# The split state of a pair-feature stage: through DRAM and back, or copied by GpSimd into a ring of half groups

## The chip, the cores and the metric

One NeuronCore of a Trainium2 chip. The metric is the device time of one execution in microseconds (us). TensorE does the matmuls, VectorE, ScalarE and GpSimd the elementwise work; SyncE only issues DMAs.

## What is computed

Four layers on a state x of 32 x 32 x 32 x 32 values, each x = x + layer(groupnorm(x)): a binarised convolution, a convolution with its own weights at every position, another binarised convolution, and the layer that the change is about:

```python
def _L3_conv_ref(x, weight, idx_a, idx_b):        # x: B, C, H, W, all 32
    cross = x[..., idx_a] * x[..., idx_b]         # all 496 pairs of the W values of a row
    feat = jnp.concatenate([x, x * x, cross], axis=-1)
    return jnp.einsum('bcij,cijo->bcio', feat, weight)   # own weights for each (c, i)
```

## The kernel before

The first three layers (some 512 us) run first and are not touched by the change, but for the table `sel` that is set up at the very start. The rest is the last stage, for layer 3.

**Layout and counts.** The state lies as 128 partitions (4 rows g of the picture x 32 columns w) by 8 parts (V) of 1024 columns (32 channels x 32 batch). A part is worked in 2 groups, a group in 4 steps (two halves of 2 steps), a step covers 4 channels, and each step has 4 feature tiles (PT): 16 groups, 64 steps, 256 tiles. A feature tile is 128 of the 512 tiled features (496 pairs and 16 squares) for 512 columns.

**The split state.** xn is the normalised part in f32. ScalarE's `high` (L573) makes its f16 upper half, VectorE's `low` (L783) the rest, both into `hi_lo`. SyncE's `put_split` (L304) writes both to DRAM (0.5 MB a part) and `get_parts` (L310) reads them back twice in four DMAs of 256 KB, so that `parts` holds on partitions 0-31 the high and 32-63 the low half, and the same again on 64-127, with the four g side by side in the columns. GpSimd's `copy_ring` (L394) copies a step's 512 columns of it to one of four slots of `ring` as soon as the gathers of four steps before are done.

**One tile.** TensorE's `gather` (L919) makes the two factors: for side a the rows 0-63 of `sel` (one-hot columns that pick a w) times rows 0-63 of the ring, into one of 2 PSUM banks; for side b rows 64-127, into one of 4 banks. ScalarE copies side a to SBUF (`left`, L605, 3 slots). VectorE multiplies side b by it (L806) into `feats` (8 slots). `mix` (L943) multiplies the 16 small matrices of the weights with the tile and sums in PSUM; f32 matmuls stand in the trace as two records each.

**TensorE's order** (`group`, L957, a hardware loop over 16 groups): at each even tile t it gathers tiles t+2 and t+3, each behind its own wait on `left_made`, then mixes t and t+1:

```python
for n in range(t + ASLOTS, t + 2 * ASLOTS) if t % ASLOTS == 0 else ():
    pe.wait_ge(left_made, j * GT + (n - ASLOTS + 1))
    gather(j, n)                                  # cut: the next group's first
```

At the first tile of a step it also waits for the step's weights and runs `own_terms` (L930, matmuls at L938), the features x and x*x, whose operands `own_x` come from GpSimd (`copy_own`, L403, copies at L414) and ScalarE (`square_own`, L580, L587).

**The other engines' orders** are written out by hand. ScalarE: `square_own` before the tiles t = 1 to 4 and t = 8 to 11 of a group, `high` of a part two ahead at t = 13 of odd groups. VectorE: `low` at t = 15 of odd groups, `add_result` (L792) at t = 3 and 11. GpSimd: two `copy_ring`, `copy_own` of four copies, the same again, and after odd groups `normalise_part` (L434, L436). SyncE: for each step it waits until the step is mixed, then loads the weights of the step four ahead (1152 KB, 4 slots), then perhaps `put_split` or `get_parts` with their waits, then writes out a half's result.

Of the kernel before, what the change touches and what calls it, by code (L numbers as in the profile page):

```python
# [6 lines left out]
F16 = mybir.dt.float16  # L7
# [6 lines left out]
P = 128  # L14
B = C = H = W = 32
G = 4
# [44 lines left out]
HCOLS = HALF * C4 * B  # L61
ASLOTS = 2
# [7 lines left out]
def build(nc, x, w_conv, bias, gamma_beta, w_pairs, mats, sel_rows, sel_index, split, out):  # L70
    ctx = ExitStack()
    with ctx:
        def sb(name, shape, dt):
            return ctx.enter_context(nc.sbuf_tensor(name, shape, dt))
# [4 lines left out]
        def sems(name, n):  # L79
            return [sem(f"{name}{i}") for i in range(n)]  # L80
# [25 lines left out]
        sel = sb("sel", [P, TILED], F16)  # L106
# [7 lines left out]
        sel_i = as_f32[:, 0:TILED].bitcast(I32)  # L114
# [5 lines left out]
        first = 2 * GCOLS  # L120
        parts = flat[:, first:first + 4 * PART].bitcast(F16).rearrange("p (s g n) -> p s g n", s=2, g=G)
        flat16 = signs.rearrange("p s n -> p (s n)")
        hi_lo = flat16[:, 0:4 * PART].rearrange("p (s k n) -> p s k n", s=2, k=2)
        ring = flat16[:, 4 * PART:4 * PART + GROUP * FCOL].rearrange("p (s n) -> p s n", s=GROUP)
# [58 lines left out]
        split_out = sems("split_out", V)  # L183
        parts_in = sems("parts_in", V)
# [78 lines left out]
        def _(sp):  # L263
# [40 lines left out]
            def put_split(i):  # L304

                sp.wait_ge(hi_split, i + 1)
                sp.wait_ge(lo_split, i + 1)
                sp.dma_start(split[i].rearrange("k p n -> p k n"), hi_lo[:, i % 2, :, :]).then_inc(split_out[i], 16)

            def get_parts(i):  # L310

                sp.wait_ge(split_out[i], 16)
                if i >= 2:
                    sp.wait_ge(ring_made, (i - 1) * KPART)
                for side in range(2):
                    for k in range(2):
                        first = (2 * side + k) * W
                        sp.dma_start(parts[first:first + W, i % 2, :, :],
                                     split[i, k].rearrange("(g w) n -> w g n", g=G)).then_inc(parts_in[i], 16)

            for i in range(2):
                put_split(i)
                get_parts(i)
            for k in range(NK):

                sp.wait_ge(mixed, PT * (k + 1))
                if k + WSLOTS < NK:
                    load_pairs(k + WSLOTS)
                grp = k // GROUP
                if k % (2 * GROUP) == 2 * GROUP - 1 and (grp + 3) // 2 < V:  # L330
                    put_split((grp + 3) // 2)
                if k % (2 * GROUP) == 0 and 2 <= grp // 2 + 1 < V:
                    get_parts(grp // 2 + 1)
                if k % HALF == 1 and k > HALF:
                    done = k // HALF
                    sp.wait_ge(result_made, 2 + done)
                    cols = slice((done - 1) * HALF * C4 * B, done * HALF * C4 * B)
                    sp.dma_start(out[:, cols], state_a[:, cols]).then_inc(out_sem, 16)
# [7 lines left out]
        def _(pool):  # L346
# [47 lines left out]
            def copy_ring(k):  # L394

                if k % (2 * GROUP) == 0 and k < NK:
                    pool.wait_ge(parts_in[k // GROUP // 2], 16 * 2 * 2)
                if k >= GROUP:
                    pool.wait_ge(gathered, (k - GROUP + 1) * PT)
                pool.tensor_copy(ring[:, k % GROUP, :].rearrange("p (g n) -> p g n", g=G),  # L400
                                 parts[:, k // KPART % 2, :, k % KPART * C4 * B:(k % KPART + 1) * C4 * B]).then_inc(ring_made, 1)

            def copy_own(grp, half):  # L403

                pool.wait_ge(part_made, grp // 2 + 1)
                if grp:
                    pool.wait_ge(own_used, GROUP * (grp - 1) + HALF * (half + 1))
                first = grp % 2 * GCOLS + half * HCOLS
                pool.wait_ge(ring_made, grp * GROUP + HALF * (half + 1))
                for g in range(G):  # L410
                    q = g % 2 * 2 * W
                    if g:
                        pool.wait_ge(own_copied, (2 * grp + half) * G + g)
# [13 lines left out]
            def normalise_part(i):  # L427
                if i >= 2:
                    pool.wait_ge(squared, 4 * G * (i - 1))
                    pool.wait_ge(hi_split, i - 1)  # L430
                    pool.wait_ge(lo_split, i - 1)
                    pool.wait_ge(own_copied, 4 * G * (i - 1))
                dst, src = (t.rearrange("p (c b) -> p c b", b=B) for t in (xn[:, i % 2, :], state_a[:, i * PART:(i + 1) * PART]))
                pool.tensor_tensor(dst, src, m_op, ALU.subtract).then_inc(part_centred, 1)  # L434
                pool.wait_ge(part_centred, i)
                pool.tensor_tensor(dst, dst, r_op, ALU.mult).then_inc(part_made, 1)  # L436

            pool.wait_ge(part_made, 1)
            normalise_part(1)
            for grp in range(NGROUP):  # L440
                copy_ring(grp * GROUP)
                copy_ring(grp * GROUP + 1)
                copy_own(grp, 0)
                copy_ring(grp * GROUP + 2)
                copy_ring(grp * GROUP + 3)
                copy_own(grp, 1)
                if grp % 2 and grp // 2 + 2 < V:
                    normalise_part(grp // 2 + 2)
            copy_ring(NK)
# [5 lines left out]
        def _(act):  # L455
# [117 lines left out]
            def high(i):  # L573

                act.wait_ge(part_made, i + 1)
                if i >= 2:
                    act.wait_ge(split_out[i - 2], 16)
                act.activation(hi_lo[:, i % 2, 0, :], xn[:, i % 2, :], ACT.Copy, scale=HALF_SCALE).then_inc(hi_split, 1)
# [14 lines left out]
            high(1)  # L593
            for n in range(TILES):
# [5 lines left out]
                if t == GT // 2 + 5 and grp % 2 and grp // 2 + 2 < V:  # L600
                    high(grp // 2 + 2)
# [8 lines left out]
        def _(dve):  # L610
# [201 lines left out]
        def _(pe):  # L812
# [106 lines left out]
            def gather(j, t):  # L919

                if t % PT == 0:
                    pe.wait_ge(ring_made, j * GROUP + (t // PT + 1))
# [20 lines left out]
            def mix(j, t):  # L943

                s = t // PT
                pe.wait_ge(feats_made, j * GT + (t + 1))
                wt = wsteps[:, s, 0:WSTEP].rearrange("p (t c g o) -> p t c g o", t=PT, c=C4, g=G)
                f = feats[:, t % FSLOTS, :].rearrange("p (g c b) -> p g c b", g=G, c=C4)
                for c in range(C4):
                    for g in range(G):  # L950
                        col = (s % HALF * C4 + c) * B
                        last = pe.matmul(psum[g * W:(g + 1) * W, 6 + s // HALF, col:col + B], wt[:, t % PT, c, g, :],  # L952
                                         f[:, g, c, :], start=False, stop=(t % (HALF * PT) == HALF * PT - 1),
                                         skip_group_check=True)
                last.then_inc(mixed, 1)

            def group(j):  # L957

                for t in range(GT):
                    for n in range(t + ASLOTS, t + 2 * ASLOTS) if t % ASLOTS == 0 else ():  # L960
                        pe.wait_ge(left_made, j * GT + (n - ASLOTS + 1))
                        if n < GT:
                            gather(j, n)
                        else:
                            gather(j + 1, n - GT)
# [9 lines left out]
                    mix(j, t)  # L975

            for t in range(ASLOTS):
                gather(0, t)
# [24 lines left out]
def _rearranged(np, inputs):  # L1003
# [14 lines left out]
    pairs3 = tiled.transpose(3, 0, 5, 4, 1, 2, 6).reshape(NK, P, WSTEP)  # L1018
# [9 lines left out]
    index = np.repeat(np.stack(sides), 2 * W, axis=0)  # L1028
# [22 lines left out]
```

## Time and profile before

| | |
|---|---|
| median of 3 runs | 794.86 us (793.28 to 800.76) |
| the profiled execution | 790.91 us, of it span 788.9 us |
| mean granted TensorE clock | 0.874 of full speed |
| busy in the span | TensorE matmuls 65%, VectorE 74%, ScalarE 62%, GpSimd 43% |
| last stage | first gather at 528.18 us, last result addition begun at 786.30 us |
| DMA from 528 to 787 us | busy share 0.94, mean 330 GB/s |
| DMAs of the split | 8 writes of 512 KB, 32 reads of 256 KB |

All times in rows are us from the start of the span, unless marked ns. The durations are those of the profiled execution; the share of busy time is that of an engine, and matmuls overlap, so a row of 64 matmuls shows the time from the first's start to the last's end. PEclk is the granted clock in tenths or as a fraction: 1.00 is 2.4 GHz, 0.50 is 1.2 GHz.

### The profile page before, as it was taken

The numbers are of one execution on the slowest core, as the hardware profiler recorded it, in microseconds if no ns is written. First come the engines' busy times: TensorE is split into PE (matmuls) and PEld (weight loads), VectorE is DVE, ScalarE is ACT, GpSimd is POOL, SyncE is SP. The second block draws the span as 40 slices with busy tenths as digits, with TensorE's granted clock in tenths as the row PEclk, the third lists the DMA queues.
The fourth block names the chain that finished last, engine by engine and source line by source line (L and its number), as shares of the span: only waits on it lengthen the run. The fifth ranks groups of instructions, "written<-read, shape, count | busy, mean of one in ns | idle before, by whom it ended". The sixth has DMA issues, their size and how long they took to land.

```text
span 788.9 us, 53642 instructions
## 1 busy us (share of the span) xinstructions
PE 510.6 (65%) x24526; PEld 385.0 (49%) x24526; DVE 581.0 (74%) x698; ACT 486.5 (62%) x836; POOL 342.0 (43%) x525
## 2 busy tenths in 40 slices
PE   0025766408489999826666605618888788787798
PEld 0025655408378888605566502204555455454555
DVE  4989899989823423379999989635878677686777
ACT  4319999674111212137999845136888788687886
POOL 1039886000445551019887103153654545545331
PEclk9997899958599999965978958957999999899999
DMA  8908999700179999905999900046999999999995
GB/s 337 398 8 310 394 396 396 282 0 1 21 272 357 375 399 401 414 28 213 391 398 395 379 8 1 0 137 215 323 363 340 389 312 394 328 334 391 321 419 184
DMA packets 45233, 217.46 MB, mean 276 GB/s; under 512 B 7040, under 2 KB 17280, under 8 KB 24704
## 3 DMA queue, kind: packets, MB, share of 16 engines
q1 hardware_dynamic: 35728, 210.06, 71.5%
q10 hardware_dynamic: 9216, 6.30, 2.6%
q0 software_dynamic: 240, 0.53, 0.2%
q8 instruction: 21, 0.34, 0.2%
q14 instruction: 28, 0.23, 0.1%
HBM read 202.18 MB, written 8.39 MB: 267 GB/s over the span
## 4 chain that ended last, share of the span: by engine, by line
PE 28%; DVE 24%; DMA 24%; ACT 8%; issue 7%; POOL 6%; ACTq 1%; SPq 1%; DVEq 0%; POOLq 0%
PE psum L843 14%; DMA wring<-in_pairs 8%; DVE stats L638 5%; DMA split<-signs 5%; PE psum L952 4%; PE psum L926 4%; DMA beyond<-state_a 3%; DMA beyond<-state_b 3%; ACT state_b L605 3%; DMA wring<-in_w 3%; POOL xn_ring L255 3%; ACT signs L476 2%; DVE xn_ring L255 2%; PE psum L853 2%; DVE state_a L766 2%
## 5 line engine op out<-in xcount | busy, mean ns | idle before, releaser
L806 DVE TENSOR_TENSOR state_b<-psum,state_b 128x512 f32<-128x512 f32 x256 | 168.0, 687 | 78.4 <-ACT state_b L605 76.5
L843 PE MATMUL psum<-signs,near 64*32 64x96 f16 (+3 forms) x6528 | 127.2, 219 | 98.7 <-DMA beyond<-nothing 38.4
L605 ACT ACTIVATE state_b<-psum 128x512 f32<-128x512 f32 x256 | 145.9, 596 | 41.9 <-PE psum L926 37.5
L843 PEld LDWEIGHTS psum<-signs,near 64*32 64x32 f16 (+1 forms) x6528 | 114.3, 104 | 107.5 <-issue 106.9
L706 DVE TENSOR_REDUCE abs_sums<-wring 128x1 f32<-128x2048 f32 x64 | 142.9, 2276 | 0.1
L476 ACT ACTIVATE signs<-wring 128x2304 f16<-128x2304 f32 x64 | 134.9, 2107 | 0.0
L926 PE MATMUL psum<-signs,sel 64*128 64x512 f16 x516 | 96.1, 407 | 38.7 <-POOL signs L400 19.3
L952 PE MATMUL psum<-state_b,wring 128*32 128x32 f32 x8192 | 106.3, 203 | 6.6 <-DVE state_b L806 3.8
L843 PE MATMUL psum<-wring,near 64*32 64x96 f32 (+5 forms) x3264 | 97.9, 243 | 16.9 <-DMA beyond<-nothing 10.6
L952 PEld LDWEIGHTS psum<-state_b,wring 128*32 128x32 f32 x8192 | 89.2, 115 | 34.6 <-issue 21.6
L843 PEld LDWEIGHTS psum<-wring,near 64*32 64x32 f32 (+1 forms) x3264 | 88.4, 109 | 24.4 <-issue 24.4
L377 POOL COPY near<-state_b 128x512 f16<-128x512 f16 (+1 forms) x64 | 33.2, 521 | 129.1 <-DVE state_b L255 65.8
L400 POOL COPY signs<-wring 128x512 f16<-128x512 f16 x65 | 39.1, 609 | 97.6 <-PE psum L926 86.4
L677 DVE STREAM_TRANSPOSE state_b<-psum 128x512 f32<-128x512 f32 x16 | 11.5, 717 | 77.1 <-PE psum L853 77.1
L843 PE MATMUL psum<-signs,beyond 32*32 32x96 f16 (+2 forms) x2176 | 65.4, 217 | 0.1
L587 ACT ACTIVATE wring<-state_b 32x256 f32<-32x256 f32 x128 | 53.1, 415 | 18.3 <-PE psum L938 15.3
L414 POOL COPY wring<-state_b 32x256 f32<-32x256 f32 x128 | 56.5, 442 | 13.0 <-POOL signs L400 4.5
L843 PEld LDWEIGHTS psum<-signs,beyond 32*32 32x32 f16 x2176 | 55.9, 102 | 5.2 <-issue 0.3
L926 PEld LDWEIGHTS psum<-signs,sel 64*128 64x128 f16 x516 | 23.0, 94 | 69.7 <-ACT state_b L605 41.2
L534 ACT ACTIVATE signs<-state_a 128x256 f32<-128x256 f32 x32 | 13.3, 417 | 59.6 <-issue 50.8
L843 PE MATMUL psum<-wring,beyond 32*32 32x96 f32 (+2 forms) x1088 | 50.0, 241 | 0.0
L843 PEld LDWEIGHTS psum<-wring,beyond 32*32 32x32 f32 x1088 | 44.0, 107 | 3.6 <-issue 0.4
(141 smaller groups left out, 834.2 us busy)
## 6 DMA issues: line engine op xcount, KB each, us to landing
wring<-in_w SPq DMA_DIRECT2D x96, 1152.0 KB, 10.2
wring<-in_pairs SPq DMA_DIRECT2D x64, 1152.0 KB, 9.0
wring<-split SPq DMA_DIRECT2D x32, 256.0 KB, 5.5
state_a<-in_x SPq DMA_DIRECT2D x8, 512.0 KB, 9.5
split<-signs SPq DMA_DIRECT2D x8, 512.0 KB, 7.8
out<-state_a SPq DMA_DIRECT2D x32, 128.0 KB, 8.7
beyond<-state_b ACTq DMA_DIRECT2D x112, 32.0 KB, 5.9
beyond<-state_a ACTq DMA_DIRECT2D x56, 32.0 KB, 6.1
```

Of the source, the lines that this page charges most:

```text
L255: return (lambda: eng.tensor_tensor(new, old, m_op, ALU.subtract)), (lambda: eng.tensor_tensor(new, new, r_op, ALU.mult))
L400: pool.tensor_copy(ring[:, k % GROUP, :].rearrange("p (g n) -> p g n", g=G), parts[:, k // KPART % 2, :, k % KPART * C4 * B:(k % KPART + 1 ...
L414: pool.tensor_copy(own_x[q:q + W, g // 2, half * HCOLS:(half + 1) * HCOLS], xn[g * W:(g + 1) * W, grp // 2 % 2, first:first + HCOLS]).then ...
L476: act.activation(signs[:, n % PIECES, :], wring[:, slot(layer, n), :], ACT.Sign).then_inc(signs_made, 1)
L587: act.activation(own_x[q:q + W, g // 2, half * HCOLS:(half + 1) * HCOLS], xn[g * W:(g + 1) * W, grp // 2 % 2, first:first + HCOLS], ACT.Sq ...
L605: act.activation(left[:, n % LSLOTS, :], psum[:, n % ASLOTS, :], ACT.Copy, scale=1.0 / HALF_SCALE / HALF_SCALE).then_inc(left_made, 1)
L638: dve.tensor_reduce(red[:, side, m * B:(m + 1) * B], blk(src, m).rearrange("p (h b) -> p b h", b=B), X, ALU.add).then_inc(gn_red[layer], 1)
L706: dve.tensor_reduce(abs_sums[:, n:n + 1], wring[:, slot(layer, n), 0:ABS_DVE], X, ALU.add, apply_absolute_value=True).then_inc(abs_made, 1)
L806: dve.tensor_tensor(feats[:, n % FSLOTS, :], psum[:, ASLOTS + n % BSLOTS, :], left[:, n % LSLOTS, :], ALU.mult).then_inc(feats_made, 1)
L843: last = pe.matmul(psum[g * B:(g + 1) * B, bank, (a * C) % 512:(a * C) % 512 + (b - a) * C], acts[q, j, s, k, :], weights[q, j, kind, s, ( ...
L926: last = pe.matmul(psum[:, bank, :], sel[half, t % PT * P:(t % PT + 1) * P], ring[half, t // PT, :], start=True, stop=True)
L952: last = pe.matmul(psum[g * W:(g + 1) * W, 6 + s // HALF, col:col + B], wt[:, t % PT, c, g, :], f[:, g, c, :], start=False, stop=(t % (HAL ...
```

## The change

The write and the reads through DRAM are gone, with `parts` and their waits. `ring` has now two slots, each for a half group (2 steps): GpSimd copies the upper half once for all 128 rows (each g on its own rows, written to two places), and then in four copies of 32 rows each the lower half of each g to the rows of its neighbour. Rows 0-63 of a slot so hold g = 0 and 1, rows 64-127 g = 2 and 3. `sel` holds both sides on all rows and is twice as wide. `gather_two` makes two tiles (the same 128 features for g = 0, 1 and for g = 2, 3) with four matmuls: side a for both row halves, then side b for both; `mix_two` mixes both. The weights of a slot are reordered to a half group and two feature tiles; their bytes and the number of matmuls stay. `high` and `low` of the next part move to t = 5 and t = 7 of odd groups, the normalisation (`centre_part`, `scale_part`) into the two halves of even groups.

```diff
--- before.py
+++ after.py
+HALVES = PART // (2 * HCOLS)
+RING_OPS = 1 + G
...
-        sel = sb("sel", [P, TILED], F16)
+        sel = sb("sel", [P, 2 * TILED], F16)
...
-        sel_i = as_f32[:, 0:TILED].bitcast(I32)
+        sel_i = as_f32[:, 0:2 * TILED].bitcast(I32)
...
-        ring = flat16[:, 4 * PART:4 * PART + GROUP * FCOL].rearrange("p (s n) -> p s n", s=GROUP)
+        ring = flat16[:, 4 * PART:4 * PART + 2 * FCOL].rearrange("p (s g n) -> p s g n", s=2, g=2)
...
-            for i in range(2):
-                put_split(i)
-                get_parts(i)
             for k in range(NK):
 
                 sp.wait_ge(mixed, PT * (k + 1))
                 if k + WSLOTS < NK:
                     load_pairs(k + WSLOTS)
-                grp = k // GROUP
-                if k % (2 * GROUP) == 2 * GROUP - 1 and (grp + 3) // 2 < V:
-                    put_split((grp + 3) // 2)
-                if k % (2 * GROUP) == 0 and 2 <= grp // 2 + 1 < V:
-                    get_parts(grp // 2 + 1)
...
+            def copy_ring(h):
+
+                i = h // (2 * HALVES)
+                if h % (2 * HALVES) == 0 and i < V:
+                    pool.wait_ge(hi_split, i + 1)
+                    pool.wait_ge(lo_split, i + 1)
+                if h >= 2:
+                    pool.wait_ge(gathered, (h - 1) * HALF * PT)
+                cols = slice(h % (2 * HALVES) * HCOLS, (h % (2 * HALVES) + 1) * HCOLS)
+                hi, lo = (hi_lo[:, i % 2, k, cols] for k in range(2))
+                pool.tensor_copy(ring[:, h % 2, :, :], hi.unsqueeze(1).to_broadcast([P, 2, HCOLS])).then_inc(ring_made, 1)
+                for g in range(G):
+                    pool.wait_ge(ring_made, RING_OPS * h + g + 1)
+                    other = g ^ 1
+                    pool.tensor_copy(ring[other * W:(other + 1) * W, h % 2, g % 2, :], lo[g * W:(g + 1) * W, :]).then_inc(ring_made, 1)
+                pool.wait_ge(ring_made, RING_OPS * (h + 1))
 
...
-                pool.wait_ge(ring_made, grp * GROUP + HALF * (half + 1))
...
+            def centre_part(i):
                 if i >= 2:
                     pool.wait_ge(squared, 4 * G * (i - 1))
                     pool.wait_ge(hi_split, i - 1)
                     pool.wait_ge(lo_split, i - 1)
                     pool.wait_ge(own_copied, 4 * G * (i - 1))
-                dst, src = (t.rearrange("p (c b) -> p c b", b=B) for t in (xn[:, i % 2, :], state_a[:, i * PART:(i + 1) * PART]))
+                dst, src = part_of(i)
                 pool.tensor_tensor(dst, src, m_op, ALU.subtract).then_inc(part_centred, 1)
                 pool.wait_ge(part_centred, i)
+
+            def scale_part(i):
+                dst, src = part_of(i)
                 pool.tensor_tensor(dst, dst, r_op, ALU.mult).then_inc(part_made, 1)
+                pool.wait_ge(part_made, i + 1)
 
             pool.wait_ge(part_made, 1)
-            normalise_part(1)
             for grp in range(NGROUP):
-                copy_ring(grp * GROUP)
-                copy_ring(grp * GROUP + 1)
+                following = grp // 2 + 1
+                copy_ring(2 * grp)
                 copy_own(grp, 0)
-                copy_ring(grp * GROUP + 2)
-                copy_ring(grp * GROUP + 3)
+                if grp % 2 == 0 and following < V:
+                    centre_part(following)
+                copy_ring(2 * grp + 1)
                 copy_own(grp, 1)
-                if grp % 2 and grp // 2 + 2 < V:
-                    normalise_part(grp // 2 + 2)
-            copy_ring(NK)
+                if grp % 2 == 0 and following < V:
+                    scale_part(following)
+            copy_ring(2 * NGROUP)
                 act.wait_ge(part_made, i + 1)
                 if i >= 2:
-                    act.wait_ge(split_out[i - 2], 16)
+                    act.wait_ge(ring_made, RING_OPS * 2 * HALVES * (i - 1))
                 act.activation(hi_lo[:, i % 2, 0, :], xn[:, i % 2, :], ACT.Copy, scale=HALF_SCALE).then_inc(hi_split, 1)
 
             def square_own(grp, half, g):
...
             high(0)
             for g in range(G):
                 square_own(0, 0, g)
-            high(1)
             for n in range(TILES):
                 grp, t = n // GT, n % GT
                 if 1 <= t <= G:
                     square_own(grp, 1, t - 1)
                 if GT // 2 <= t < GT // 2 + G and grp + 1 < NGROUP:
                     square_own(grp + 1, 0, t - GT // 2)
-                if t == GT // 2 + 5 and grp % 2 and grp // 2 + 2 < V:
-                    high(grp // 2 + 2)
+                if t == G + 1 and grp % 2 and grp // 2 + 1 < V:
+                    high(grp // 2 + 1)
             low(0)
-            low(1)
             for n in range(TILES):
                 grp, t = n // GT, n % GT
-                if t == GT // 2 + 7 and grp % 2 and grp // 2 + 2 < V:
-                    low(grp // 2 + 2)
+                if t == G + 3 and grp % 2 and grp // 2 + 1 < V:
+                    low(grp // 2 + 1)
+            def gather_two(j, t):
+
+                half, tile = t // (GT // 2), t // 2 % PT
+                if t % (GT // 2) == 0:
+                    pe.wait_ge(ring_made, j * (2 * RING_OPS) + RING_OPS * (half + 1))
                 for side in range(2):
-                    half = slice(side * 2 * W, (side + 1) * 2 * W)
-                    bank = (0, ASLOTS)[side] + t % (ASLOTS, BSLOTS)[side]
-                    last = pe.matmul(psum[:, bank, :], sel[half, t % PT * P:(t % PT + 1) * P],
-                                     ring[half, t // PT, :], start=True, stop=True)
-                last.then_inc(gathered, 1)
+                    for u in range(2):
+                        rows = slice(u * 2 * W, (u + 1) * 2 * W)
+                        bank = (0, ASLOTS)[side] + (t + u) % (ASLOTS, BSLOTS)[side]
+                        last = pe.matmul(psum[:, bank, :], sel[rows, side * TILED + tile * P:side * TILED + (tile + 1) * P],
+                                         ring[rows, half, :, :], start=True, stop=True)
+                        if side == 1:
+                            last.then_inc(gathered, 1)
+            def mix_two(j, t):
+
+                half, tile = t // (GT // 2), t // 2 % PT
+                pe.wait_ge(feats_made, j * GT + (t + 2))
+                wt = wsteps[:, t // PT, 0:WSTEP].rearrange("p (t s c g o) -> p t s c g o", t=2, s=HALF, c=C4, g=G)
+                f = [feats[:, (t + u) % FSLOTS, :].rearrange("p (g s c b) -> p g s c b", g=2, s=HALF, c=C4) for u in range(2)]
+                for s in range(HALF):
+                    for c in range(C4):
+                        for g in range(G):
+                            col = (s * C4 + c) * B
+                            last = pe.matmul(psum[g * W:(g + 1) * W, 6 + half, col:col + B], wt[:, tile % 2, s, c, g, :],
+                                             f[g // 2][:, g % 2, s, c, :], start=False, stop=(tile == PT - 1),
+                                             skip_group_check=True)
+                last.then_inc(mixed, 2)
 
             def group(j):
 
-                for t in range(GT):
-                    for n in range(t + ASLOTS, t + 2 * ASLOTS) if t % ASLOTS == 0 else ():
-                        pe.wait_ge(left_made, j * GT + (n - ASLOTS + 1))
-                        if n < GT:
-                            gather(j, n)
-                        else:
-                            gather(j + 1, n - GT)
+                for t in range(0, GT, 2):
+                    pe.wait_ge(left_made, j * GT + (t + 2))
+                    if t + 2 < GT:
+                        gather_two(j, t + 2)
+                    else:
+                        gather_two(j + 1, 0)
                     if t % (GT // 2) == 0:
                         half = t // (GT // 2)
                         pe.wait_ge(own_copied, j * 2 * G + G * (half + 1))
...
                         pe.wait_ge(pairs_in[t // PT], j * 16 + 16)
                         pe.sem_inc(step_begun, 1)
                         own_terms(t // PT)
-                    mix(j, t)
-
-            for t in range(ASLOTS):
-                gather(0, t)
+                    mix_two(j, t)
+
+            gather_two(0, 0)
...
-    pairs3 = tiled.transpose(3, 0, 5, 4, 1, 2, 6).reshape(NK, P, WSTEP)
+    tiled = tiled.reshape(C // C4 // HALF, HALF, C4, G, V, 2, 2, P, W)
+    pairs3 = tiled.transpose(4, 0, 5, 7, 6, 1, 2, 3, 8).reshape(NK, P, WSTEP)
...
-    index = np.repeat(np.stack(sides), 2 * W, axis=0)
+    index = np.repeat(np.concatenate(sides)[None], P, axis=0)
```

## Rows read from the trace of the kernel before

**Rows 1.** The page, chain that ended last: share of the span by engine
```profile
PE 28%; DVE 24%; DMA 24%; ACT 8%; issue 7%; POOL 6%; ACTq 1%; SPq 1%; DVEq 0%; POOLq 0%
```

**Rows 2.** Groups of instructions, 514 to 787 us: busy, mean ns | idle before, releasers
```profile
L806 DVE TENSOR_TENSOR state_b<-psum,state_b 128x512 f32<-128x512 f32 x256 | 168.0, 687 | 78.4 <-ACT state_b L605 76.5 <-PE psum L952 0.7
L605 ACT ACTIVATE state_b<-psum 128x512 f32<-128x512 f32 x256 | 145.9, 596 | 41.9 <-PE psum L926 37.5
...
L414 POOL COPY wring<-state_b 32x256 f32<-32x256 f32 x128 | 56.5, 442 | 13.0 <-POOL signs L400 4.5 <-PE psum L938 2.3
...
L400 POOL COPY signs<-wring 128x512 f16<-128x512 f16 x65 | 39.1, 609 | 97.6 <-PE psum L926 86.4 <-DMA wring<-split 10.9
```

**Rows 3.** Timeline of TensorE: own terms that open the steps 0, 4, 40, 44, 45, 48
```profile
531.12 0.65 PE L938 MATMUL psum<-wring 64*32 64x32 f32 x32
...
551.20 0.46 PE L938 MATMUL psum<-wring 64*32 64x32 f32 x32
...
696.91 0.46 PE L938 MATMUL psum<-wring 64*32 64x32 f32 x32
...
710.98 0.46 PE L938 MATMUL psum<-wring 64*32 64x32 f32 x32
716.75 0.66 PE L938 MATMUL psum<-wring 64*32 64x32 f32 x32 [2.21 <-DMA wring<-in_pairs]
...
729.23 0.46 PE L938 MATMUL psum<-wring 64*32 64x32 f32 x32
```

**Rows 4.** Windows of 4 us: busy of each engine (x), PEclk, DMA share, GB/s
```profile
710.00:714.00 4.00, 3.53 (x170) 2.11 (x168) 2.85 (x6) 3.85 (x8) 0.89 (x1) 1.00 1.05 300
...
718.00:722.00 4.00, 3.92 (x194) 2.37 (x186) 1.64 (x3) 2.89 (x6) 3.19 (x7) 0.74 1.02 422
```

**Rows 5.** Timeline of SyncE's DMA queue: start, us spent issuing
```profile
704.10 1.75 SPq L318 DMA_DIRECT2D wring<-split  x4
705.89 0.43 SPq L269 DMA_DIRECT2D wring<-in_pairs  x1
```

**Rows 6.** Timeline near the end of the stage, all engines
```profile
773.14 0.60 ACT L605 ACTIVATE state_b<-psum 128x512 f32<-128x512 f32 x1
...
773.77 0.41 ACT L587 ACTIVATE wring<-state_b 32x256 f32<-32x256 f32 x1
...
773.80 0.39 PE L926 MATMUL psum<-signs,sel 64*128 64x512 f16 x2 [0.24 <-ACT state_b L605]
774.20 0.60 ACT L605 ACTIVATE state_b<-psum 128x512 f32<-128x512 f32 x1
...
778.87 0.61 PE L926 MATMUL psum<-signs,sel 64*128 64x512 f16 x4
779.30 2.32 ACT L605 ACTIVATE state_b<-psum 128x512 f32<-128x512 f32 x4 [0.75 <-PE psum L926]
...
779.40 0.76 PE L952 MATMUL psum<-state_b,wring 128*32 128x32 f32 x64
...
782.38 1.09 ACT L605 ACTIVATE state_b<-psum 128x512 f32<-128x512 f32 x2 [0.77 <-PE psum L926]
```

**Rows 7.** Timeline at the start and at the end of the stage
```profile
514.63 1.06 ACT L578 ACTIVATE signs<-state_b 128x1024 f16<-128x1024 f32 x1 [3.44 <-DVE state_b L781]
...
515.79 2.31 DVE L786 SCALAR_TENSOR_TENSOR signs<-state_b,signs 128x1024 f16<-128x1024 f32 x1 [1.19 <-ACT signs L578]
...
528.18 1.04 PE L926 MATMUL psum<-signs,sel 64*128 64x512 f16 x4 [19.33 <-POOL signs L400]
...
786.30 0.42 DVE L792 TENSOR_TENSOR state_a<-psum,state_a 128x256 f32<-128x256 f32 x1 [0.72 <-PE psum L952]
```

**Rows 8.** Timeline of a later `low` and the copies beside it
```profile
726.07 1.21 DVE L786 SCALAR_TENSOR_TENSOR signs<-state_b,signs 128x1024 f16<-128x1024 f32 x1
726.11 2.79 POOL L414 COPY wring<-state_b 32x256 f32<-32x256 f32 x4 [0.16 <-POOL signs L400]
```

**Rows 9.** Timeline of the head of the kernel
```profile
11.00 0.48 DVE L635 TENSOR_SCALAR sel<-signs,row_id 128x512 f16<-128x512 int32 x1 [10.00 <-DMA bias<-in_b]
```

More of the change, by code:

```diff
@@ L67, with build @@
 PILED = 5
-def build(nc, x, w_conv, bias, gamma_beta, w_pairs, mats, sel_rows, sel_index, split, out):
+def build(nc, x, w_conv, bias, gamma_beta, w_pairs, mats, sel_rows, sel_index, out):
     ctx = ExitStack()
@@ L119, in build @@
         own_x = flat[:, 0:2 * GCOLS].rearrange("p (u n) -> p u n", u=2)
-        first = 2 * GCOLS
-        parts = flat[:, first:first + 4 * PART].bitcast(F16).rearrange("p (s g n) -> p s g n", s=2, g=G)
         flat16 = signs.rearrange("p s n -> p (s n)")
         hi_lo = flat16[:, 0:4 * PART].rearrange("p (s k n) -> p s k n", s=2, k=2)
-        ring = flat16[:, 4 * PART:4 * PART + GROUP * FCOL].rearrange("p (s n) -> p s n", s=GROUP)
+        ring = flat16[:, 4 * PART:4 * PART + 2 * FCOL].rearrange("p (s g n) -> p s g n", s=2, g=2)
         feats = state_b[:, 0:FSLOTS * FCOL].rearrange("p (s n) -> p s n", s=FSLOTS)
@@ L182, in build @@
         squared = sem("squared")
-        split_out = sems("split_out", V)
-        parts_in = sems("parts_in", V)
         ring_made = sem("ring_made")
@@ L302, in _ @@
             signed(2 * CHUNKS - 1)
[L304 to L319, printed above, removed]
-            for i in range(2):
-                put_split(i)
-                get_parts(i)
             for k in range(NK):
@@ L392, in _ @@
                     copy_near(layer, n)
[L394 to L401, printed above, removed]
+            def copy_ring(h):
[13 more added lines that the diff above has]
+                pool.wait_ge(ring_made, RING_OPS * (h + 1))
             def copy_own(grp, half):
@@ L425, in _, with part_of @@
             m_op, r_op = (t[:, 0:B].unsqueeze(1).to_broadcast([P, C, B]) for t in (mean, rstd))
-            def normalise_part(i):
+            def part_of(i):
+                return (t.rearrange("p (c b) -> p c b", b=B) for t in (xn[:, i % 2, :], state_a[:, i * PART:(i + 1) * PART]))
+            def centre_part(i):
                 if i >= 2:
@@ L917, in _ @@
             pe.wait_ge(sel_made, 1)
-            def gather(j, t):
-                if t % PT == 0:
-                    pe.wait_ge(ring_made, j * GROUP + (t // PT + 1))
+            def gather_two(j, t):
+                half, tile = t // (GT // 2), t // 2 % PT
+                if t % (GT // 2) == 0:
+                    pe.wait_ge(ring_made, j * (2 * RING_OPS) + RING_OPS * (half + 1))
                 for side in range(2):
-                    half = slice(side * 2 * W, (side + 1) * 2 * W)
-                    bank = (0, ASLOTS)[side] + t % (ASLOTS, BSLOTS)[side]
-                    last = pe.matmul(psum[:, bank, :], sel[half, t % PT * P:(t % PT + 1) * P],
-                                     ring[half, t // PT, :], start=True, stop=True)
-                last.then_inc(gathered, 1)
+                    for u in range(2):
[5 more added lines that the diff above has]
+                            last.then_inc(gathered, 1)
             def own_terms(s):
@@ L941, in own_terms @@
                 last.then_inc(own_used, 1)
[L943 to L955, printed above, removed]
@@ L1043 @@
          for k, v in arrays.items()}
-    split = nc.dram_tensor("split", (V, 2, P, PART), F16, kind="Internal").ap()
     out = nc.dram_tensor("out_0", (P, STATE), F32, kind="ExternalOutput").ap()
     build(nc, a["x"], [a["w0"], a["w1"], a["w2"]], [a["b0"], a["b2"]], a["gb"], a["pairs3"], a["mats"],
-          a["row"], a["index"], split, out)
+          a["row"], a["index"], out)
     r = run(nc, [{f"in_{k}": v for k, v in arrays.items()}], core_ids=[0])
```

## The prediction

> **What bounds the kernel now.** I read the chain that ended last first: TensorE 28%, VectorE 24%, DMA 24% [rows 1]. The DMA share is no average matter, it comes in a pattern that the timeline of TensorE shows when one looks only at the own terms that open a step. Four steps from 696.91 to 710.98 take 14.07 us; the next four, to 729.23, take 18.25 [rows 3]. The slow four begin with 2.21 us in which TensorE waits for the weights of a step. Before that wait, SyncE issued its four reads of the split state ahead of the next weights [rows 5]; the DMA engines are fully busy there, and after it the granted clock is down, 0.74 in the mean of 718 to 722 us [rows 4], so a part of these steps runs at 1.2 GHz. That happens once in each of the parts: TensorE's own-term rows have five such stalls above 2 us, and one of 1.60.
>
> In the undisturbed 14.07 us ScalarE sets half the pace. In its line a tile with a square costs 1.06 us from one `left` (773.14) to the next (774.20), with 0.60 for the `left` and 0.41 for the square [rows 6]. Eight tiles of a group have a square: 8.5 us. The other eight take 5.6 us and are bound by TensorE: ScalarE does four of them in 2.32 us and then idles 0.75 [rows 6]. VectorE follows: 78.4 us idle, nearly all behind `left` [rows 2]. So ScalarE and TensorE are already close; what lets them overlap is that tile t+2 is gathered while ScalarE still copies tile t+1, because each gather waits for one bank only.
>
> **The change, part by part.**
>
> *The double wait.* `gather_two` starts only when both banks of side a are free, and ScalarE can copy nothing until it is through with three of its four matmuls (side a twice, side b once). Between two pairs nothing overlaps, so the cycle is a sum. From the end of a `left` (773.74) to the gather that it frees (773.80): 0.06. From a gather's start to the `left` behind two matmuls: 0.43 (778.87 to 779.30); four last 0.61 where two last 0.39, and since the row halves run side by side the third ends with the fourth: 0.22 more, 0.65. Two `left`: 1.09 [rows 6]. A pair without a square: 0.06 + 0.65 + 1.09 = 1.80 us. Of the squares at t = 1 to 4 and 8 to 11, those at even t fall into the gather's 0.71 us and are hidden; those at odd t stand between two `left`: 0.06 + 0.65 + 1.06 + 0.60 = 2.37 us. A group has four pairs of each kind: 16.7 us against 14.07. Does TensorE fit beneath? After the gather's 0.53 (778.87 to 779.40, rows 6) it has own terms and the mix, 0.46 and 0.76 at most, 1.75 in all; the product of the second tile, 0.69 after its `left` [rows 2], ends about when the gather does. It fits by a hair, and an end too late by 0.1 would show only in the eight pairs of a step's start without squares. Sixteen groups: +2.6 x 16 = +42 us.
>
> Bounds: no gap at all (ScalarE hides it, -0.71 in each pair without a square and -0.3 in one with) is the old cadence, +0; every gather at the low clock, 1.04 for four matmuls [rows 7], gives +0.43 in each of 128 pairs, +55 on top. I take the rows at the high clock, since the stretch with 1.06 us a tile from 710 to 714 us kept 1.00 [rows 4] though TensorE idled in every pair.
>
> *Round trip gone at the start.* Now `high` ends at 515.69, `low` lasts 2.31 beside GpSimd's normalisation, and the first gather is at 528.18 [rows 7]. After: `low` alone takes 1.21 as in [rows 8], to 517.0; the wide ring copy 0.61 and four narrow ones at 0.44 [rows 2] with 0.16 between, so the first gather at 519.6: -8.6 us. The narrow f16 copy appears in no row; bounds 0.3 to 0.61 each, +-0.7 us.
>
> *Weights' stalls gone.* 12.6 MB less for the queue, and SyncE's loads stand behind no put or get. At 4.2 us a step the loads of 1152 KB (2.8 us at the 422 GB/s of [rows 4]) have room. Nothing but the weights and the results remains, and I count no stall and no low clock after one. Late next is the gather's wait above.
>
> *Split in the loop.* `high` (1.06, rows 7) stands between the `left` of tiles 4 and 5: +1.08. `low` before tile 7 makes that product 1.2 us late; TensorE is then 0.3 behind the square pair that follows. 1.4 us in each of 7 parts, +9.8. Now the same costs about 1.0, inside the 18.25.
>
> *GpSimd.* Per half one ring fill 0.61 + 0.16 + 4 x 0.44 = 2.5, `copy_own` 1.9, in even groups 2.4 of normalisation: 6.8 us in a half of 8.3. The ring copy is released when the gathers of the half before last are through, one half before it is needed, so it has some 7.6 us for its own 2.5. Its cover is the half; if it went, each us over 8.3 would be on the path.
>
> The trace shows the port between GpSimd and VectorE: four own copies take 2.79 us beside a `low` of 1.21 [rows 8], where the mean is 0.44 each, and the first `low` took 2.31 beside GpSimd [rows 7]. By the Trainium skill (SBUF — State Buffer, "Who interferes with whom") a VectorE instruction with two SBUF inputs contends with a GpSimd instruction that reads SBUF, one with at most one does not. The trace agrees, since the product, with one factor in PSUM, stays at 0.69. By that rule the new copies would be slowed by the eight `low` alone.
>
> *Table.* `sel` doubles: VectorE's 0.48 us becomes about 0.96, and 256 KB more, 0.6 at 422 GB/s, land before the last constants, for which it waits until 11.00 [rows 9]. All layers stand behind this. Between +0 and +1.5, I take +1.0.
>
> **The sum.** Last stage from first gather to last mix: now 528.18 to 786.30 [rows 7], 258.1 us. After: 16 x 16.7 = 266.9; less 1.1, as the last group has no squares for a next one; +9.8; +1.4 for the last pair, whose product and mix lie behind no other pair; and a slow first group. That one now takes 531.12 to 551.20, 20.1 us, 6.0 above the undisturbed [rows 3], by the low clock and TensorE's own gaps; I carry the 6.0 over (3 to 9). Sum 283.0. It begins at 519.6 and ends at 802.6, 16.3 later than now; with the table +17.3. The profiled execution's 790.9 becomes 808.2. The median of the runs is 3.95 above that execution: 794.86 + 17.3 = 812 us.
>
> The Trainium skill has a rule that speaks against this change (Perfetto Trace Analysis, "Matmuls"): independent matmul groups should rotate through PSUM banks so that one is evacuated while the next is computed. By that rule the two banks of side a would be worth the overlap that I priced at 42 us; with only its half true it would be 21 us, and the sum 791.
>
> **The rivals.**
>
> *Old cadence stays, faster.* The gather's 0.71 us would hide behind squares and slack as the undisturbed groups' ScalarE idle of 0.75 does now; only the stalls and the round trip go. Then 812 - 42 = 770 us. For it: ScalarE is idle 41.9 us behind TensorE [rows 2]. Against: that idle follows four copies in a row, which the code no longer allows. It decides once a mean pair takes under 1.95 us instead of 2.09.
>
> *Half the gap.* If the third matmul ends clearly before the fourth, at 0.50, each pair is 0.13 to 0.15 shorter: -18 us, 794, no change.
>
> *GpSimd becomes the bound.* If narrow copies cost twice the 0.44, ring 4.3 + own 3.7 + 2.4 = 10.4 against 8.3 in the even groups' halves: +2.1 x 16 = +33, 845 us. Against: the 0.44 is of the same 32 x 256 shape.
>
> *The clock.* Each `high` and `low` opens two gaps of some 1.4 us on TensorE. Stalls of 2.2 us were followed by the low clock, that of 1.60 was not. A drop in each part for two pairs is +6, 818; the low clock nearly throughout +55, 867.
>
> **Chances.** Forecast with its own spread of 802 to 822, 0.62; clock drops, to 832, 0.10; GpSimd or a lasting low clock 0.07; half the gap 0.09; old cadence 0.12. The range 788 to 832 leaves out the old cadence and the worst two. A measurement of this kernel tells about 1% from no change. Faster by over 1%: 0.13, within 1%: 0.09, slower: 0.78.
>
> **What would show it.** Steps without squares near 3.6 us and with them 4.7, ScalarE idle about 0.7 behind L926's successor in each pair, no wait for `in_pairs`, a first gather near 520 us, groups near 16.7 us. Groups at 14 us would make the forecast wrong; GpSimd waits ahead of the gather would make it the ring.

## The result and the profile after

The changed kernel takes 806.84 us (median of 4 runs, 805.12 to 809.87) against 795.52 us: ratio 1.0155, 95% interval 1.0085 to 1.0225. A second comparison gave 1.0142 (1.0080 to 1.0204). The forecast was 812, slower; the sign and the mechanism held, the size was forecast at 17.3 us where 11.3 were measured. The four runs of the kernel before spread from 793.28 to 800.76, and its profiled execution took 790.91, less than any of them; the changed kernel's profiled one took 806.27.

The chain that ended last has lost most of its DMA, and ScalarE and "issue" have grown where [rows 1] had 8% and 7%:

```profile
DVE 28%; PE 22%; ACT 18%; issue 13%; DMA 9%; POOL 7%; ACTq 2%; DVEq 0%; POOLq 0%
```

The own terms that open the steps 12, 13, 14 and 16 show two things at once: no wait for `in_pairs` as at 716.75 in [rows 3], and a group of 18.00 us, 1.3 of it for `high` and `low`:

```profile
578.56 0.45 PE L927 MATMUL psum<-wring 64*32 64x32 f32 x32
...
583.77 0.46 PE L927 MATMUL psum<-wring 64*32 64x32 f32 x32
...
588.21 0.46 PE L927 MATMUL psum<-wring 64*32 64x32 f32 x32
...
596.56 0.45 PE L927 MATMUL psum<-wring 64*32 64x32 f32 x32
```

The group before, from 561.93 to 578.56, has neither and takes 16.63; from then on every such group takes 16.7, where [rows 3] had 14.07. TensorE's gathers inside it (own terms and mixes left out), and then ScalarE's timeline:

```profile
569.67 0.60 PE L914 MATMUL psum<-signs,sel 64*128 64x512 f16 x4 [0.84 <-ACT state_b L592]
...
572.02 0.60 PE L914 MATMUL psum<-signs,sel 64*128 64x512 f16 x4 [0.67 <-ACT state_b L592]
...
573.80 0.60 PE L914 MATMUL psum<-signs,sel 64*128 64x512 f16 x4 [0.29 <-ACT state_b L592]
```

```profile
570.31 0.60 ACT L592 ACTIVATE state_b<-psum 128x512 f32<-128x512 f32 x1 [0.25 <-PE psum L914]
570.93 0.41 ACT L575 ACTIVATE wring<-state_b 32x256 f32<-32x256 f32 x1
571.37 0.60 ACT L592 ACTIVATE state_b<-psum 128x512 f32<-128x512 f32 x1
572.66 1.09 ACT L592 ACTIVATE state_b<-psum 128x512 f32<-128x512 f32 x2 [0.69 <-PE psum L914]
```

Read them against each other: the `left` that starts at 571.37 ends at 571.97, the gather begins at 572.02, and the next `left` not before 572.66. In that 0.69 us ScalarE has nothing to do, and before each gather TensorE has nothing to do either (0.84, 0.67, 0.29). From gather to gather it is 2.35 us with a square between the copies; of the four pairs of a group without one, two take 1.78 (572.02 to 573.80) and two 1.87 (573.80 to the next gather at 575.67). The groups of instructions say the same in total; compare [rows 2]:

```profile
L792 DVE TENSOR_TENSOR state_b<-psum,state_b 128x512 f32<-128x512 f32 x256 | 171.2, 689 | 96.6 <-ACT state_b L592 95.3
L592 ACT ACTIVATE state_b<-psum 128x512 f32<-128x512 f32 x256 | 146.4, 596 | 76.3 <-PE psum L914 74.8
...
L381 POOL COPY signs<-signs 32x256 f16<-32x256 f16 x132 | 52.0, 394 | 8.1
```

ScalarE's idle time behind TensorE has doubled, from 37.5 to 74.8 us. The weights now land in 5.4 us (median) after their issue, where it was 9.0.

The start of the stage went as intended, from the start of `high` to the first gather 5.13 us instead of the 13.55 of [rows 7], and `low` is back at 1.23 as GpSimd does nothing beside it:

```profile
513.28 1.06 ACT L566 ACTIVATE signs<-state_b 128x1024 f16<-128x1024 f32 x1 [3.44 <-DVE state_b L768]
...
514.45 1.23 DVE L773 SCALAR_TENSOR_TENSOR signs<-state_b,signs 128x1024 f16<-128x1024 f32 x1 [1.20 <-ACT signs L566]
515.83 0.61 POOL L377 COPY signs<-signs 128x512 f16<-128x512 f16 x1 [22.04 <-DVE signs L773]
516.50 1.76 POOL L381 COPY signs<-signs 32x256 f16<-32x256 f16 x4
...
518.41 1.03 PE L914 MATMUL psum<-signs,sel 64*128 64x512 f16 x4 [10.90 <-POOL signs L381]
```

The head, against [rows 9]: the constants come 0.65 us later, the table takes VectorE 0.75 us instead of 0.48, and the first reduction starts 0.92 us later (12.32 instead of 11.40).

So the spans of the two profiled executions add up: +0.9 at the head, -2.3 in the three layers between (the change does not touch them; the unaltered changed kernel, profiled again, reached the first own terms 2.0 us later than this one, so that much is spread), -8.4 up to the first gather, and +25.4 in the stage (518.41 to 801.87, 283.5 us, against 258.1). Together +15.6, from 788.9 to 804.5.

### The profile page after: what moved, and what is told of

Its sections match the earlier page's. It is cut to its first block, busy times and chain, and to the rows that moved or that the text cites. A ratio compares the mean times of both kernels' runs of the same rounds, so it can differ in the third digit from the quotient of the medians.

```text
span 804.5 us, 53537 instructions
## 1 busy us (share of the span) xinstructions
PE 496.5 (62%) x24526; PEld 369.3 (46%) x24526; DVE 583.0 (72%) x698; ACT 486.8 (61%) x836; POOL 368.2 (46%) x625
## 4 chain that ended last, share of the span: by engine, by line
DVE 28%; PE 22%; ACT 18%; issue 13%; DMA 9%; POOL 7%; ACTq 2%; DVEq 0%; POOLq 0%
PE psum L829 12%; ACT state_b L592 9%; DVE state_b L792 7%; DVE stats L625 5%; PE psum L914 4%; ACT signs L464 4%; POOL xn_ring L253 3%; ACT wring L575 3%; DMA wring<-in_w 3%; DMA beyond<-state_a 2%; DMA beyond<-state_b 2%; DVE xn_ring L253 2%; PE psum L839 2%; ACTq L480 2%; DVE state_a L753 2%
## 5 line engine op out<-in xcount | busy, mean ns | idle before, releaser
L792 DVE TENSOR_TENSOR state_b<-psum,state_b 128x512 f32<-128x512 f32 x256 | 171.2, 689 | 96.6 <-ACT state_b L592 95.3
L592 ACT ACTIVATE state_b<-psum 128x512 f32<-128x512 f32 x256 | 146.4, 596 | 76.3 <-PE psum L914 74.8
L914 PE MATMUL psum<-signs,sel 64*128 64x512 f16 x516 | 82.1, 398 | 73.4 <-ACT state_b L592 59.4
L942 PE MATMUL psum<-state_b,wring 128*32 128x32 f32 x8192 | 100.0, 201 | 18.7 <-DVE state_b L792 8.3
L942 PEld LDWEIGHTS psum<-state_b,wring 128*32 128x32 f32 x8192 | 85.2, 112 | 52.3 <-DVE state_b L792 47.9
L829 PE MATMUL psum<-wring,near 64*32 64x96 f32 (+5 forms) x3264 | 95.4, 240 | 16.6 <-DMA beyond<-nothing 10.6
L829 PEld LDWEIGHTS psum<-wring,near 64*32 64x32 f32 (+1 forms) x3264 | 86.0, 107 | 23.7 <-issue 23.7
L377 POOL COPY signs<-signs 128x512 f16<-128x512 f16 x33 | 20.1, 609 | 128.0 <-DVE signs L773 69.4
L914 PEld LDWEIGHTS psum<-signs,sel 64*128 64x128 f16 x516 | 15.0, 95 | 90.6 <-ACT state_b L592 67.9
L381 POOL COPY signs<-signs 32x256 f16<-32x256 f16 x132 | 52.0, 394 | 8.1
L394 POOL COPY wring<-state_b 32x256 f32<-32x256 f32 x128 | 50.3, 393 | 7.9
```

Source lines behind the costliest of these rows:

```text
L381: pool.tensor_copy(ring[other * W:(other + 1) * W, h % 2, g % 2, :], lo[g * W:(g + 1) * W, :]).then_inc(ring_made, 1)
L592: act.activation(left[:, n % LSLOTS, :], psum[:, n % ASLOTS, :], ACT.Copy, scale=1.0 / HALF_SCALE / HALF_SCALE).then_inc(left_made, 1)
L792: dve.tensor_tensor(feats[:, n % FSLOTS, :], psum[:, ASLOTS + n % BSLOTS, :], left[:, n % LSLOTS, :], ALU.mult).then_inc(feats_made, 1)
L829: last = pe.matmul(psum[g * B:(g + 1) * B, bank, (a * C) % 512:(a * C) % 512 + (b - a) * C], acts[q, j, s, k, :], weights[q, j, kind, s, ( ...
L914: last = pe.matmul(psum[:, bank, :], sel[rows, side * TILED + tile * P:side * TILED + (tile + 1) * P], ring[rows, half, :, :], start=True, ...
L942: last = pe.matmul(psum[g * W:(g + 1) * W, 6 + half, col:col + B], wt[:, tile % 2, s, c, g, :], f[g // 2][:, g % 2, s, c, :], start=False, ...
```

## The experiments

**ScalarE released by side a alone.** On the changed kernel:

```diff
-                        if side == 1:
-                            last.then_inc(gathered, 1)
+                        last.then_inc(gathered if side == 1 else left_ready, 1)
...
-                act.wait_ge(gathered, n + 1)
+                act.wait_ge(left_ready, n + 1)
...
                 dve.wait_ge(left_made, n + 1)
+                dve.wait_ge(gathered, n + 1)
```

> The changed kernel, but ScalarE's copy waits for the matmul of side a alone (a semaphore of its own); VectorE also waits for side b. Theory (the serial cycle of gather and copies sets the group): the gap shrinks from 0.06 + 0.65 to 0.06 + 0.43 us, a pair takes 1.58 without and 2.15 with a square, a group 14.9 instead of 16.7, the kernel about 28 us less, 779. Rival (the narrow ring copies or the reordered matmuls set the pace): no change, 807.

781.55 us, ratio to the kernel before 0.9804 (0.9748 to 0.9860). The gap fell from 0.69 to 0.48 us:

```profile
588.59 0.60 PE L916 MATMUL psum<-signs,sel 64*128 64x512 f16 x4
589.01 1.09 ACT L593 ACTIVATE state_b<-psum 128x512 f32<-128x512 f32 x2 [0.48 <-PE psum L916]
```

An undisturbed group takes 15.0 us. The 0.22 us per pair that the third matmul was priced at are worth 25 us over 128 pairs, 28 had been expected.

**One wait for each bank, in the new layout.** Each tile of a pair is gathered whole, behind the wait for its own bank:

```diff
-                for side in range(2):
-                    for u in range(2):
+                for u in range(2):
+                    if waits:
+                        pe.wait_ge(left_made, waits[u])
+                    for side in range(2):
```

> The changed kernel, but each tile of a pair is gathered behind its own wait for one bank, side a and side b of it one after the other on the same row half. Theory: the overlap is back, a tile with a square costs 1.06 us again; without squares TensorE's pair is gather 0.86 + mix 0.69 + own terms 0.2 = 1.75; a group 15.5, the kernel some 19 us less, 788. Rival (overlap does not matter): the serial row halves make it slower than 807.

781.09 us, ratio 0.9825 (0.9764 to 0.9886), a group 15.2 us: 26 us come back. Where the tiles have squares the overlap is back; ScalarE starts `left` every 1.06 us and waits for nothing in between:

```profile
627.48 0.60 ACT L592 ACTIVATE state_b<-psum 128x512 f32<-128x512 f32 x1
...
628.54 0.60 ACT L592 ACTIVATE state_b<-psum 128x512 f32<-128x512 f32 x1
```

The price is on TensorE: the two sides of a tile now lie on the same row half, and two such matmuls take 0.60 us (at 627.34) where two on different halves took 0.39 [rows 6]. The run does not give the overlap's worth by itself, since the edit also lets ScalarE start behind two matmuls instead of three, which alone gave 25 us above. Nor does it say whether the 1.1 us by which a group is longer than 14.07 belong to the matmuls on one row half or to `mix_two`, which waits for two products at once.

**The double wait put into the kernel before.**

```diff
-                    for n in range(t + ASLOTS, t + 2 * ASLOTS) if t % ASLOTS == 0 else ():
-                        pe.wait_ge(left_made, j * GT + (n - ASLOTS + 1))
+                    if t % ASLOTS == 0:
+                        pe.wait_ge(left_made, j * GT + (t + ASLOTS))
+                    for n in range(t + ASLOTS, t + 2 * ASLOTS) if t % ASLOTS == 0 else ():
```

> The kernel before, but both gathers of a pair stand behind the wait for both banks; nothing else. Theory: pairs of 1.58 and 2.15 us, an undisturbed group 14.9 instead of 14.1, +8 to +14 us (the stalls for weights absorb some): 804 to 809. Rival (ScalarE's idle time covers the wait): no change, 795.

792.71 us, ratio 0.9963 (0.9920 to 1.0006). The expectation missed: no loss, though the undisturbed groups did lengthen to 15.2 us. Taken alone this run would have acquitted the double wait. Its trace does not show where the loss went: it is of the longest of the ten executions, 801.66 us, with four waits for weights, 10.0 us together, where the trace of the kernel before has six with 15.4 us. Two runs without the round trips say what the double wait costs.

**The kernel before without its round trips.** The calls of `put_split` and `get_parts` in the loop go, with the waits on them:

```diff
-                if k % (2 * GROUP) == 2 * GROUP - 1 and (grp + 3) // 2 < V:
-                    put_split((grp + 3) // 2)
-                if k % (2 * GROUP) == 0 and 2 <= grp // 2 + 1 < V:
-                    get_parts(grp // 2 + 1)
...
-                if k % (2 * GROUP) == 0 and k < NK:
+                if k % (2 * GROUP) == 0 and k < 4 * GROUP:
                     pool.wait_ge(parts_in[k // GROUP // 2], 16 * 2 * 2)
...
-                if i >= 2:
+                if 2 <= i < 4:
                     act.wait_ge(split_out[i - 2], 16)
```

> The kernel before without the write and the reads of the parts 2 to 7 of the split state; the ring is filled from what parts 0 and 1 left (the features of these parts are so of other data). Theory: the stalls for weights and the low clock after them go, eight steps take 29.2 instead of 32.5 us, -20 us: 775. Rival (the weights alone fill the DMA queues): under -5 us.

769.47 us (767.52 to 769.96), ratio 0.9654 (0.9599 to 0.9709). There is no wait for `in_pairs` left, and eight steps take 29.3 us. The round trips inside the loop so cost 25.7 us. The spread of the runs shrank with them, from 13 us (13 runs) to 2.4 (4 runs; 3.7 in the ten runs of the next kernel, which also lacks them).

**The same with the double wait.** The diff of the double wait on that kernel.

> The kernel before without the write and reads of parts 2 to 7 of the split state (their features are of other data), and with both gathers of a pair behind the wait for both banks. Against the run without the round trips, 769.5 us. Theory: without stalls nothing absorbs the double wait, groups 15.2 instead of 14.1, 769.5 + 17 = 786. Rival (the wait itself is free, as the timed comparison of the double wait alone seems to say): 770.

788.25 us (785.98 to 789.71), 18.8 above the 769.47, and the two ranges do not touch. (The two were measured on different chips, on which the kernel before took 795.15 and 795.50 us.) Groups are 15.2 us where they were 14.1. Without the round trips ScalarE makes four copies in a row (first line); with the double wait it idles 0.49 us between two pairs (second line):

```profile
624.88 2.23 ACT L601 ACTIVATE state_b<-psum 128x512 f32<-128x512 f32 x4
...
640.03 1.09 ACT L601 ACTIVATE state_b<-psum 128x512 f32<-128x512 f32 x2 [0.49 <-PE psum L922]
```

So the double wait does cost, as soon as nothing else holds TensorE up. The four medians together: the round trips in the loop cost 25.7 us without the double wait (795.15 against 769.47) and 4.5 us with it (792.71 against 788.25). Whichever of the two is there hides most of the other.

**The squares before the even tiles.** On the changed kernel and, as a check, on the kernel before:

```diff
-                if 1 <= t <= G:
-                    square_own(grp, 1, t - 1)
-                if GT // 2 <= t < GT // 2 + G and grp + 1 < NGROUP:
-                    square_own(grp + 1, 0, t - GT // 2)
+                if t % 2 == 0 and t < GT // 2:
+                    square_own(grp, 1, t // 2)
+                if t % 2 == 0 and t >= GT // 2 and grp + 1 < NGROUP:
+                    square_own(grp + 1, 0, (t - GT // 2) // 2)
```

> The changed kernel, but ScalarE's eight squares of a group stand before the even tiles 0, 2, ... 14 instead of before 1 to 4 and 8 to 11, so that each falls into the gap of 0.71 us in which ScalarE waits for a gather. Theory (the cycle of gather and two copies is serial): every pair takes 1.80 us, a group 14.4 instead of 16.7, -37 us: 770. Rival (ScalarE's total work sets the group): no change, 807.

777.47 us, ratio 0.9780 (0.9707 to 0.9852): 29 us less than the changed kernel for moving eight instructions in each group. A group takes 14.56, 3.64 for each of its steps. The squares stand in the gap and cost nothing; ScalarE does the same work as before, so its total did not set the group. Of the missing 8 us of the expected 37, most is found: `high` and `low` now cost 1.8 us in a part instead of 1.3, since no square pair behind them gives slack, and a pair takes 1.82 instead of 1.80.

> The kernel before with the squares before even tiles. Theory: ScalarE's pair with one square takes 1.6 us, an undisturbed group 12.9 instead of 14.1; but weights and split state together want 27.5 us of DMA in eight steps, so the stalls grow and eight steps take 29 to 31 us instead of 32.5: -12 to -25 us, 775. Rival: the stalls eat all of it, 795.

794.86 us, ratio 0.9962 (0.9911 to 1.0014). The expectation missed and the rival held. The last group without a wait takes 12.7 us, so ScalarE's order no longer sets it, and the gain is given back at the weights, in five parts twice instead of once. In the trace (of an execution of 797.87 us, near the top of its ten, 785.87 to 798.36) the waits for weights add up to 27.4 us against 15.4, and the mean granted clock from 560 us to the end of the stage is 0.89 against 0.95. Own terms and the wait before them:

```profile
611.09 0.46 PE L938 MATMUL psum<-wring 64*32 64x32 f32 x32 [1.72 <-DMA wring<-in_pairs]
618.24 0.65 PE L938 MATMUL psum<-wring 64*32 64x32 f32 x32 [3.22 <-DMA wring<-in_pairs]
```

This and the double wait are the same finding from two sides: a cost added and a cost removed on the engines both vanish in the kernel before. For the cost added, the runs without the round trips show that the loads hide it; the even squares were not run without them, so for the cost removed it rests on the longer waits of this trace.

**Both edits on the changed kernel.**

> Both edits on the changed kernel: squares before even tiles, and ScalarE released by side a alone. Theory: the gap of 0.49 us just holds a square of 0.41, a pair takes 1.58 us, a group 12.7, -64 us: 743; the weights of a group, 4.7 MB, then want 390 GB/s, so stalls may give back up to 10 us. Rival as above: no better than either edit alone, 770 to 781.

760.31 us (759.25 to 761.46), ratio 0.9558 (0.9487 to 0.9629), faster than both kernels: 46 us under the changed one. Expected were 743. A group takes 13.4 instead of 12.7, and the timeline points to the next limit, which no run tests: TensorE's mix now waits for VectorE's product (33 times, 21.1 us together from 555 to 750 us), and `low`, and at 608.77 `add_result`, stand before products that it waits for:

```profile
604.54 1.22 DVE L774 SCALAR_TENSOR_TENSOR signs<-state_b,signs 128x1024 f16<-128x1024 f32 x1
...
606.42 0.76 PE L943 MATMUL psum<-state_b,wring 128*32 128x32 f32 x64 [1.28 <-DVE state_b L794]
```

No wait for weights shows, although 345 GB/s are moved from 560 to 740 us.

**GpSimd's ring copies made twice.** The rival in which GpSimd sets the pace, tested by more of its work:

```diff
-RING_OPS = 1 + G
+RING_OPS = 1 + 2 * G
...
-                for g in range(G):
-                    pool.wait_ge(ring_made, RING_OPS * h + g + 1)
+                for n in range(2 * G):
+                    g = n % G
+                    pool.wait_ge(ring_made, RING_OPS * h + n + 1)
```

> The changed kernel with the four narrow copies of each ring half made twice, 1.8 us more of GpSimd in each of 33 fills. Theory (GpSimd has a half's 8.3 us and needs 6.8 in even and 4.4 in odd groups): even groups run 0.3 us over and catch up in odd ones; only the very first fill is on the path, +1.8, in all +2 to +4 us: 810. Rival (the ring's copies set the pace): +1.8 in every half, +50 us or more: 860.

806.29 us; the unaltered kernel on the same chip 805.64:

> The changed kernel unaltered, on the chip of the run above. Expected of every theory: its ratio to the kernel before again near 1.0155, 1.010 to 1.020.

Ratios 1.0158 (1.0093 to 1.0223) and 1.0142 (1.0080 to 1.0204). 33 x 1.8 = 58 us more of GpSimd are worth under a microsecond, and the steps take 4.22 and 4.13 us as before. The 1.8 us of the first fill do show: from the start of `high` to the first gather it is 6.94 us against 5.11 in the unaltered kernel; the two stages differ by 1.3 us the other way (281.7 and 282.9), within what the executions spread. The rival that GpSimd's ring copies set the pace is out.

## Why the prediction was right, and by how much it was off

*The double wait, +42 us.* Right, mechanism and size: group 16.7 forecast and measured, pairs 2.37 and 1.80 forecast, 2.35 and a mean of 1.83 measured (two at 1.78, two at 1.87), so that two deviations of under 0.03 us cancel. It consists of two parts that the runs separate: the wait for both banks (+18.8 us alone, without the round trips) and the later release by side b in third place (25 us). The first was shown with the matmuls in the old order, the second on the changed kernel; together they are 44, near the 42.

*The round trip at the start, -8.6 us.* Measured -8.4. The narrow copies cost 0.39 to 0.44 each, at the middle of the bounds.

*The weights' stalls gone.* Right that they go, and no other wait took their place. This is the mis-sized term. The forecast's terms imply their cost in one execution: its stage of 258.1 us less a stall-free 237.0 (16 groups of 14.07, 6.0 for the first, 1.0 for each later `high` and `low`, less the 1.1 of the last group) = 21.1 us. For that execution the sum holds: the stage was forecast at 283.0 us and took 283.5, and the spans differ by 15.6 us where 17.3 were forecast, less mostly by the 2.3 us of the untouched layers. The step that failed in size is the last one, where the difference of two executions was carried over to the median of the runs. The profiled execution of the kernel before lay 4.6 us under the median of 795.52, that of the changed kernel only 0.6 under its 806.84. With and without the round trips in the loop the profiled executions differ by 21.1 us (790.91 and 769.77), the medians by 25.7. With 25.7 in place of 21.1 the forecast would have been 12.7 us over the median, 11.3 were measured. That the stalls are what varies between the executions of the kernel before is borne out by the runs without round trips, which lie within 2.4 and 3.7 us instead of 13; that they were shorter than usual in the profiled execution is not shown, since there is no second trace of this kernel.

*`high` and `low`, +1.4 in each of seven parts:* 1.3. *The table, +1.0:* 0.9. *The slow first group, 6.0:* from step 0 to step 4 it took 21.0 us, 4.4 above 16.7, and the next group another 0.8 beside its `high` and `low`. The first group began at the low clock (granted 0.50 from 520 to 527 us) and met it again (0.56 from 538 to 541). *GpSimd's room:* held, even with 1.8 us more for each half. The slowing beside VectorE that the prediction gave the new copies did not arise: GpSimd waits for `low` before it copies, and all 132 narrow copies of the ring took 0.39 to 0.40 us. *The clock:* the rival of a drop in each part did not come about; the gaps of 1.3 to 1.4 us at `high` and `low` were followed by the low clock in two of seven parts, at 548 and 688 us (granted clock 0.64 and 0.65 in the 4 us from there), with some 0.8 us lost at each.

*The rivals.* Old cadence stays: refuted by the 16.7 us. Half the gap: refuted, from gather to copy it is 0.64 us (572.02 to 572.66) where 0.65 was forecast. The rule of the Trainium skill (Perfetto Trace Analysis, "Matmuls") that banks should rotate so that one is evacuated while the next is computed had been weighed at 42 us. The runs bear the rule out and price it lower: one wait for both banks costs 18.8 us where no stall hides it, and the rest of the 42 is the later release.

## What to carry to other kernels

When a change joins two steps of a pipeline to save instructions or waits, write down the cycle between the two engines before and after: with two buffers freed and refilled as one, the cycle is the sum of the refill, up to the point where it releases the other engine, and of the emptying of both buffers. A part tried alone on a kernel that waits for its loads may say nothing of its cost; take the loads' stall away first, and then add the part. And an execution whose time has a stall in it is one draw of it, so take the size of a stall from the median of several runs.

## What the runs showed that was not expected

The kernel before was held by its loads more than its profile tells: 1.1 us more in each undisturbed group and 1.4 us less both left its time where it was, within 0.9%. One DMA wait of 1.6 to 3.7 us in six of the eight parts was the visible end of that. And the narrow GpSimd copy of 32 x 256 values takes 0.39 us in f16 as in f32, half the bytes at the same price, where the wide one with four times the rows and twice the values a row takes 0.61.
